# Maxima of a cross-attention's scores in the two row halves of the array, and its weighted sum in one PSUM bank

## The chip, the cores and the metric

One core of one Trainium2 chip. The metric is the device time of one execution in microseconds (us). Three runs of the kernel before took 4037.01, 4039.97 and 4041.73 us; the median is 4039.97.

## The reference

The program is a stack of four layers on `x` (32 batches, 56 tokens, 128 features), each a cross-attention and a feed-forward part; layer 3's cross-attention also has a self-attention ahead of it. All four cross-attentions read the same context `ctx_512` (32 batches, 1500 keys, 64 features), with 16 heads. Cut to what matters, layer 0 is

```
qh = (norm(x) @ Wq) by head;  kh = (ctx @ Wk) by head;  vh = (ctx @ Wv) by head
attn = softmax(qh . kh * scale)          # over 1500 keys
x    = x + (attn . vh) by head @ Wo + bo
x    = x + ffn(norm(x))
```

Layers 1 to 3 differ in head size, biases and in a normalised context (layer 3). The four cross-attentions are called cross 0 to cross 3 here; the kernel's index for them is `ci`.

## The kernel before

**Folding.** `Wk` is folded into `Wq` and `Wv` into `Wo` ahead of each cross-attention, so every head has 64 query features that meet the raw context, and 64 output features. For a batch there are 16 x 56 = 896 rows (head, token), in 7 groups of 128 (`NJ`), and 1500 keys in 12 tiles of 125 (`KT`, `KP`). fp32 values are split into two bf16 halves, high and low.

**Operands of the scores.** The keys of a batch lie in `cs` (128 partitions: 64 high halves above 64 low halves), the high halves once more in `chx` (64 partitions, and a 65th full of ones). The queries lie in `Qh` (high halves, twice, on partitions 0 to 63 and 64 to 127) and `Ql` (64 low halves, and the row's shift, minus its maximum, on the 65th). A score tile, 125 keys by 448 rows, is two matmuls into one bank (L619, L622): `cs` against `Qh` (128 rows), and `chx` against `Ql` (65 rows).

**Maxima.** The softmax's shift needs a rough maximum over the keys for each row. The 1500 keys are taken as three lots of 500, called s, r and the difference d = first lot minus second (`diff`, made by VectorE in `keys`, L777). For each of the 7 groups `product` (L588) makes three 128 x 500 products: d, s and r, 21 in a batch. ScalarE takes relu(d) (`relu`, L687), VectorE adds s to it and takes the maximum in one instruction, which is the larger of the first two lots, and takes the maximum of r by itself (`reduce`, L762). The 7 shifts per row block are turned by TensorE, copied, and sent by DMA to `Ql`'s 65th row.

**Steps.** One stage is a loop over steps `T`, 12 per batch, 384 in all, written out for each engine; every engine takes its work of a step in the order of the code. `turns` (L355) gives the maxima products of a step, for a batch 17 steps ahead, from the table `PLAN` (L359): up to two items, a first and a second. TensorE's order within a step (`pe_cross`, from L602) is: the first product; four score matmuls; the second product; the weighted sum of the tile two steps back; and in some steps a projection of queries (24 matmuls of 56 columns, 32 in cross 2), 7 transposes, or half of the output projection (`slot`, L417). ScalarE: relu of the first item, two exponentials of 125 x 448, relu of the second. VectorE: the first item's maximum, the low halves of the exponentials (L817), the second item's. GpSimd: the rest of these low halves (L539) and the finishing of a batch.

**Banks.** The products take banks 0 and 1 in turn (in a stage's first batch 0 to 3), so that each waits until the last but one has been read (`wait_max_bank`, L401). The scores take banks 2 to 4 in turn. The weighted sum has columns 2620 to 3522, in banks 5 and 6: for each of the 7 groups 129 columns, which are 64 features by the high half, the denominator, and 64 features by the low half. Bank 7 serves the rest.

**Weighted sum** (L628 to L647): for each group one matmul with the high halves of the exponentials as weights and 129 columns of `cnb`, and one with the low halves and 65 columns. The fourth group meets the bank's end at column 3072, so that its 129 columns are cut into 65 and 64: 15 matmuls in all. After the last tile of a batch ScalarE copies the 903 columns to `raw` in two pieces (L724, L725); GpSimd adds the two features' parts, divides, and splits the result into high and low halves (L546 to L564).

**Copies.** SyncE sends a batch's projected queries from `qch` and `qcl` to `Qh` (four DMAs, L389 and L390) and `Ql` (two, L392 and L393); the products wait for the first four, the scores for all six.

Of the kernel before, what the change touches and what calls it, by code (L numbers as in the profile page):

```python
# [22 lines left out]
EPS = 1e-5  # L23
TWICE = 6
E, F = 8, 256
RND = 12582912.0

# [14 lines left out]
def build(nc, a, out):  # L42
    with ExitStack() as ctx:
# [39 lines left out]
        Ql = big[:, 7168:14336].bitcast(BF16).rearrange("p (b n) -> p b n", b=HB)  # L83
        O = big[:, 14336:21504].bitcast(BF16).rearrange("p (b j c) -> p b j c", b=HB, j=NJ)
# [7 lines left out]
        chx = [cx[0:65, 2250 + 750 * i:3000 + 750 * i].bitcast(BF16) for i in range(2)]  # L92
# [5 lines left out]
        raw = [wst[:, 4032 + 903 * i:4935 + 903 * i].rearrange("p (j c) -> p j c", j=NJ) for i in range(2)]  # L98
# [256 lines left out]
        def turns(T):  # L355
            k, n = divmod(T + 17, KT)
            return [(k, PLAN[n])] if 0 <= k < B else []
# [3 lines left out]
        ORDER = tuple(i for two in PLAN for i in two if i)  # L361
        PARTS = {"d": 0, "s": 1, "r": 2}

        def before(item, kinds):
            return sum(i[0] in kinds for i in ORDER[:ORDER.index(item)])

        def halves(kb, item):
            return NJ * kb + before(item, "d")

        def maxima(kb, item):  # L370
            return 2 * NJ * kb + before(item, "sr")

        def products_to(kb, item):
            return len(ORDER) * kb + ORDER.index(item)
# [8 lines left out]
        def sp_spread(y, w, ci, k):  # L383
# [17 lines left out]
        def wait_max_bank(w, kb, k, item):  # L401
            n = ORDER.index(item)
            if k == 0 and n < 4:
                if kb:
                    w.wait_ge(s["red"], maxima(kb, ORDER[0]))
# [1928 lines left out]
```

## Time and profile before

| | |
|---|---|
| time, median of 3 | 4039.97 us |
| profiled execution: span, first to last instruction | 4037.7 us |
| TensorE matmuls, busy | 3793.1 us (94%), 43467 of them |
| TensorE weight loads, busy | 2886.6 us (71%) |
| VectorE, busy | 3135.7 us (78%) |
| ScalarE, busy | 2674.0 us (66%) |
| GpSimd, busy | 2544.9 us (63%) |
| mean granted TensorE clock | 0.954 |

The profiled execution is another one than the three timed; the profile gives its span, and no time of its own beyond that. In the rows below PE is TensorE, PEld its weight loads, DVE VectorE, ACT ScalarE, POOL GpSimd, SPq the DMA queue of SyncE. `ps<-cx,wst` is an instruction that writes `ps` from `cx` and `wst`; `125*128 125x65` is 125 rows by 128 columns of weights, and 65 moving columns on 125 rows; x15 is how many follow one another. A matmul's duration is its latency, not its share of the engine: matmuls overlap, so the distance between two starts is what one takes from TensorE. `[0.20 <-DVE wst L772]` is idle time before the instruction and what ended it. Nearly all matmuls go through the helper at L186, so groups are told apart by their tiles and shapes.

### The profile page before, as it was taken

What the parts mean: (1) busy time and instruction counts of PE and PEld (TensorE: products, weight loads), DVE (VectorE), ACT (ScalarE), POOL (GpSimd) and SP (SyncE); (2) the same over time, 40 slices, a digit from 0 to 9 for tenths busy, and PEclk for the clock granted to TensorE, in tenths of its full rate; (3) what the DMA queues carried; (4) which work ended last, traced back from release to release, by engine and by line L of the source; (5) the groups of instructions that cost most, each with busy time, mean ns of one, the idle gap of its engine ahead of it and who ended that gap; (6) DMA issues with size and microseconds to landing.
All of it is one profiled execution on the core that took longest, in us unless ns stands there. A gap on an engine that the chain in (4) does not pass through costs nothing.

```text
span 4037.7 us, 110587 instructions
## 1 busy us (share of the span) xinstructions
PE 3793.1 (94%) x43467; PEld 2886.6 (71%) x43467; DVE 3135.7 (78%) x6499; ACT 2674.0 (66%) x5365; POOL 2544.9 (63%) x2457
## 2 busy tenths in 40 slices
PE   6999999989969999999799999996997899999987
PEld 4777777766637777777577777775765677777765
DVE  6999999858978888888577888886654788888864
ACT  4888887756637777777467777773442577777752
POOL 4888888759856776767456676675001476676761
PEclk8999999979989999999699999998998899999988
DMA  4333333125432222121112212110000212122100
GB/s 129 104 110 112 110 108 107 41 92 158 143 100 61 57 60 61 54 61 49 28 54 62 59 54 64 57 54 21 3 1 18 64 54 64 57 59 61 55 22 15
DMA packets 157328, 266.80 MB, mean 66 GB/s; under 512 B 26632, under 2 KB 97432, under 8 KB 155432
## 3 DMA queue, kind: packets, MB, share of 16 engines
q1 hardware_dynamic: 156360, 259.67, 22.5%
q8 instruction: 343, 5.62, 0.6%
q14 instruction: 177, 1.45, 0.1%
q10 hardware_dynamic: 448, 0.06, 0.0%
HBM read 165.10 MB, written 50.26 MB: 53 GB/s over the span
## 4 chain that ended last, share of the span: by engine, by line
PE 87%; DVE 6%; POOL 2%; ACT 2%; DMA 1%; issue 1%; SPq 1%; POOLq 0%; DVEq 0%; ACTq 0%
PE ps L186 83%; PE ps L659 1%; DVE xn L166 1%; POOL wst L539 1%; PE ps L242 1%; PE ps L255 1%; PE ps L1638 1%; DVE wst L817 1%; DVE wst L772 0%; PE ps L1160 0%; DVE st L151 0%; DMA big<-big 0%; DVE relu L769 0%; DMA ynN<-cx 0%; ACT wb L324 0%
## 5 line engine op out<-in xcount | busy, mean ns | idle before, releaser
L539 POOL TENSOR_TENSOR wst<-wst 125x384 bf16<-125x384 f32 (+1 forms) x1536 | 1432.0, 932 | 843.4 <-ACT wst L745 783.1
L745 ACT ACTIVATE wst<-ps 125x448 f32<-125x448 f32 x3072 | 1518.5, 553 | 569.3 <-PE ps L186 554.8
L186 PE MATMUL ps<-big,cx 128*125 128x448 bf16 (+1 forms) x6144 | 1428.8, 354 | 0.8 <-DMA big<-topT 0.8
L186 PEld LDWEIGHTS ps<-cx,wst 125*128 125x128 bf16 x23040 | 1113.5, 98 | 307.5 <-POOL wst L539 15.2
L817 DVE TENSOR_TENSOR wst<-wst 125x512 bf16<-125x512 f32 (+1 forms) x1536 | 1269.4, 827 | 56.8 <-ACT wst L745 56.5
L186 PE MATMUL ps<-cx,wst 125*128 125x65 bf16 (+2 forms) x23040 | 1202.4, 204 | 12.1 <-POOL wst L539 11.6
L186 PEld LDWEIGHTS ps<-big,cx 128*125 128x125 bf16 (+1 forms) x6144 | 835.1, 137 | 284.2 <-issue 1.8
L186 PE MATMUL ps<-cx,big 128*128 128x500 bf16 (+1 forms) x2688 | 709.4, 317 | 10.2 <-DVE big L1743 2.6
L772 DVE TENSOR_REDUCE wst<-ps 128x1 f32<-128x500 f32 x896 | 603.9, 674 | 136.6 <-PE ps L186 123.9
L769 DVE CUSTOM_DVE_ANT_0 wst<-ps,wst 128x500 bf16<-128x500 f32 x448 | 302.6, 676 | 207.2 <-PE ps L186 150.8
L769 DVE CUSTOM_DVE_ANT_0 relu<-ps,relu 128x500 bf16<-128x500 f32 x448 | 301.8, 674 | 147.8 <-PE ps L186 84.1
L186 PE MATMUL ps<-diff,big 128*128 128x500 bf16 x896 | 343.5, 383 | 33.7 <-DMA big<-big 20.8
L693 ACT ACTIVATE wst<-ps 128x500 bf16<-128x500 f32 x448 | 270.9, 605 | 67.5 <-PE ps L186 67.5
L693 ACT ACTIVATE relu<-ps 128x500 bf16<-128x500 f32 x448 | 269.2, 601 | 40.5 <-PE ps L186 39.6
L182 POOL TENSOR_TENSOR rs<-ve,mhalf 128x8 f32<-128x8 f32 x26 | 43.1, 1656 | 394.2 <-DVE ve L161 380.3
L186 PEld LDWEIGHTS ps<-cx,big 128*128 128x128 bf16 x2688 | 202.2, 97 | 79.4 <-DVE wst L772 19.4
L564 POOL TENSOR_TENSOR big<-wst,big 128x448 bf16<-128x448 f32 x124 | 173.8, 1402 | 9.7
L186 PE MATMUL ps<-big 128*128 128x448 bf16 (+2 forms) x832 | 162.2, 353 | 4.4 <-POOL big L1055 2.3
L734 ACT ACTIVATE xn<-ps 128x896 bf16<-128x896 bf16 x128 | 122.3, 956 | 49.0 <-PE ps L659 48.4
L546 POOL TENSOR_TENSOR wst<-wst 128x448 f32<-128x448 f32 x124 | 146.0, 1177 | 9.7
L186 PEld LDWEIGHTS ps<-diff,big 128*128 128x128 bf16 x896 | 88.1, 98 | 83.1 <-DMA big<-big 21.4
L552 POOL TENSOR_TENSOR wst<-wst,rden 128x448 f32<-128x448 f32 x124 | 139.9, 1128 | 9.7
(250 smaller groups left out, 4260.2 us busy)
## 6 DMA issues: line engine op xcount, KB each, us to landing
big<-big SPq DMA_DIRECT2D x768, 56.0 KB, 2.7
cx<-ctxT SPq DMA_DIRECT2D x96, 375.0 KB, 3.5
cx<-ctxN SPq DMA_DIRECT2D x64, 377.9 KB
cx<-in_ctxN SPq DMA_DIRECT2D x64, 375.0 KB
cx<-ctxT SPq DMA_DIRECT2D x96, 187.5 KB, 3.8
ctxN<-cx SPq DMA_DIRECT2D x32, 377.9 KB
ynN<-cx SPq DMA_DIRECT2D x32, 377.9 KB
cx<-ynN SPq DMA_DIRECT2D x32, 377.9 KB
```

The costliest lines, as they stand in the source:

```text
L182: g.tensor_tensor(rs[:, cols], ve[:, cols], mhalf[:, cols], ALU.pow).then_inc(s["pw"], 1)
L186: return t.matmul(o, l, r, start=start, stop=stop, skip_group_check=True)
L539: g.tensor_tensor(pl[r][0:KP, at:], pf[r][0:KP, at:], pf[r][0:KP, at:].bitcast(BF16)[:, 1::2], ALU.subtract).then_inc(s["plp"], 1)
L546: g.tensor_tensor(r, r, raw[u][:, :, C + 1:], ALU.add).then_inc(s["fp"], 1)
L552: g.tensor_tensor(r, r, per_row(rden[u][:, :], C), ALU.mult).then_inc(s["fp"], 1)
L564: g.tensor_tensor(O[:, k % HB, :, C:], r, O[:, k % HB, :, 0:C], ALU.subtract).then_inc(s["fp"], 1)
L693: e.activation(relus[n % 2], bank(max_bank(kb, k, item), 500), ACT.Relu).then_inc(s["half"], 1)
L734: e.activation(ob[p % 2][:, :, 64 * r:64 * r + NQ], bank(7).bitcast(BF16)[:, 0:HQ].rearrange("c (h q) -> c h q", h=H), ACT.Copy).then_inc( ...
L745: e.activation(pf[T % 3][0:KP, cols], bank(2 + n2 % 3, 448)[0:KP], ACT.Exp, scale=scale).then_inc(s["ev"], 1)
L769: v.tensor_tensor_reduce(out=half, in0=of, in1=half, scale=1.0, scalar=-3.0e38, op0=ALU.add, op1=ALU.max, accum_out=to[:, j, 0:1]).then_in ...
L772: v.tensor_reduce(to[:, j, 1:2], of, AX.X, ALU.max).then_inc(s["red"], 1)
L817: v.tensor_tensor(pl[r][0:KP, 0:to], pf[r][0:KP, 0:to], pf[r][0:KP, 0:to].bitcast(BF16)[:, 1::2], ALU.subtract).then_inc(s["pl"], 1)
```

## The change

The halves are laid out anew. `cs` holds the high halves of the keys twice, and `chx` zeros with a row of ones on partitions 0 to 63 and the low halves on 64 to 127. `Qh` and `Ql` get the names `Q1` (high above low halves) and `Q2` (shift in partition 0 of a block of zeros, high halves on 64 to 127). The score matmuls become `cs` against `Q1` and `chx` against `Q2`, both with 128 rows. Maxima use only the high halves of the keys: a pair of products runs on 64 rows each, one on partitions 0 to 63 with `Q1`, one on 64 to 127 with `Q2`, into two banks; a product that is alone in its step has 128 rows. `PLAN` has 9 pairs and 3 singles for a batch, all at the start of the step, ahead of the scores; the products take banks 0, 1 and 6 in turn. The weighted sum has 65 columns per group in bank 5 alone, and adds the features' low part onto the same columns by a matmul of its own: 21 matmuls, one copy by ScalarE, no addition by GpSimd. Products wait for all six query copies.

```diff
-        PLAN = (("d0", "s0"), ("r0", "d1"), ("s1", "d2"), ("r1", ""), ("s2", "r2"), ("d3", "s3"),
-                ("r3", "d4"), ("s4", "d5"), ("r4", "s5"), ("r5", "d6"), ("s6", ""), ("r6", ""))
...
+        PLAN = (("d0", "r0"), ("d1", "s0"), ("r1", "r2"), ("d2", "s1"), ("d3", "s2"), ("r3",),
+                ("d4", "s3"), ("d5", "s4"), ("r4", "r5"), ("d6", "s5"), ("s6",), ("r6",))
...
+        TILES = (slice(0, 64), slice(64, 128))
...
-        def max_bank(kb, k, item):
-            n = products_to(kb, item)
-            return n % 2 if k else ORDER.index(item) % 4
...
+        def max_bank(k, n, u):
+            return (0, 1, 6)[(through(n - 1, "dsr") + u) % 3] if k else 2 * (n % 2) + u
...
-            for r in (0, 64):
-                y.dma_start(Qh[r:r + 64, o, 0:HQ // 2], qch[u][0:64]).then_inc(s[f"qd_{u}"], 16)
-                y.dma_start(Qh[r:r + 64, o, HQ // 2:], qch[u][64:128]).then_inc(s[f"qd_{u}"], 16)
+            for of, rows in ((Q1, TILES[0]), (Q2, TILES[1])):
+                y.dma_start(of[rows, o, 0:HQ // 2], qch[u][0:64]).then_inc(s[f"qd_{u}"], 16)
+                y.dma_start(of[rows, o, HQ // 2:], qch[u][64:128]).then_inc(s[f"qd_{u}"], 16)
...
-            y.dma_start(Ql[0:64, o, 0:HQ // 2], qcl[u][0:64]).then_inc(s[f"ql_{u}"], 16)
-            y.dma_start(Ql[0:64, o, HQ // 2:], qcl[u][64:128]).then_inc(s[f"ql_{u}"], 16)
+            y.dma_start(Q1[64:128, o, 0:HQ // 2], qcl[u][0:64]).then_inc(s[f"ql_{u}"], 16)
+            y.dma_start(Q1[64:128, o, HQ // 2:], qcl[u][64:128]).then_inc(s[f"ql_{u}"], 16)
...
                 if k < B:
-                    y.dma_start(cs[i], srcT[k]).then_inc(s[f"lT_{i}"], 16)
+                    for rows in TILES:
+                        y.dma_start(cs[i][rows, :], srcT[k][0:64]).then_inc(s[f"lT_{i}"], 16)
...
-            for k in range(2):
-                g.memset(chx[k][64:65, :], 1.0).then_inc(s["zo"], 1)
-                w.wait_ge(s["zo"], zeroed(ci - 1) + k + 1)
+            if ci in (0, 3):
+                g.memset(cx[0:64, 2250:3750], 0.0).then_inc(s["zo"], 1)
+                w.wait_ge(s["zo"], zeroed(ci - 1) + 1)
+                g.memset(cx[0:1, 2250:3750], ONES).then_inc(s["zo"], 1)
+                w.wait_ge(s["zo"], zeroed(ci - 1) + 2)
...
+            g.memset(big[0:64, 7168:7168 + QB * HQ // 2], 0.0).then_inc(s["zo"], 1)
...
-                if 0 <= (k := due(T, KT + 4)) < B - 1:
-                    u, kb = k % 2, B * ci + k
-                    r = raw[u][:, :, 0:C]
-                    w.wait_ge(s["fc"], 2 * (kb + 1))
-                    g.tensor_tensor(r, r, raw[u][:, :, C + 1:], ALU.add).then_inc(s["fp"], 1)
-                    w.wait_ge(s["fp"], 4 * kb + 1)
...
-            def product(k, item):
-                kind, j = item[0], int(item[1])
+            def products_of(k, n):
+                items = PLAN[n]
                 wait_spread_high(w, ci, k)
+                wait_spread_low(w, ci, k)
                 wait_keys(w, ci, k)
                 w.wait_ge(s["dif"], b0 + k + 1)
-                wait_max_bank(w, b0 + k, k, item)
-                c = PARTS[kind]
-                mm(t, bank(max_bank(b0 + k, k, item), 500), Qh[:, k % QB, 128 * j:128 * j + 128],
-                   diff[:, :] if kind == "d" else cs[k % 3][:, 500 * c:500 * c + 500], True, True).then_inc(s["mxm"], 1)
+                wait_max_banks(w, b0 + k, k, n)
+                for u, item in enumerate(items):
+                    c, j = PARTS[item[0]], int(item[1])
+                    rows = TILES[u] if len(items) == 2 else slice(0, 128)
+                    r = mm(t, bank(max_bank(k, n, u), 500), (Q1, Q2)[u][rows, k % QB, 128 * j:128 * j + 128],
+                           diff[rows, :] if c == 0 else cs[k % 3][rows, 500 * c:500 * c + 500], True, True)
+                r.then_inc(s["mxm"], len(items))
 
...
                     n2 += 1
-                for k, items in turns(T):
-                    if items[0]:
-                        product(k, items[0])
+                for k, n in turns(T):
+                    products_of(k, n)
...
                         w.wait_ge(s["ev"], evac + n2 - 2)
-                        mm(t, o, cs[k % 3][:, keys], Qh[:, k % QB, cols], True, False)
+                        mm(t, o, cs[k % 3][:, keys], Q1[:, k % QB, cols], True, False)
                         wait_shift(w, ci, k)
-                        wait_spread_low(w, ci, k)
-                        mm(t, o, chx[k % 2][:, keys], Ql[0:65, k % QB, cols], False, True).then_inc(s["sc"], 1)
+                        mm(t, o, chx[k % 2][:, keys], Q2[:, k % QB, cols], False, True).then_inc(s["sc"], 1)
                         n2 += 1
-                for k, items in turns(T):
-                    if items[1]:
-                        product(k, items[1])
                 if 0 <= T - 2 < NT:
                     k, i = divmod(T - 2, KT)
                     r = (T - 2) % 3
                     ph = pf[r][0:KP, :].bitcast(BF16)[:, 1::2]
                     w.wait_ge(s["pl"], t0 + T - 1)
                     wait_values(w, ci, k)
-                    if k:
-                        w.wait_ge(s["fc"], 2 * (b0 + k) - 1)
+                    w.wait_ge(s["fc"], b0 + k)
                     for j in range(NJ):
-                        if k and j == 3:
-                            w.wait_ge(s["fc"], 2 * (b0 + k))
                         if j == JP[ci]:
                             w.wait_ge(s["plp"], NT * ci + T - 1)
                         cols = slice(128 * j, 128 * j + 128)
-                        at = 2620 + 129 * j
-                        n = min(129, 3072 - at) if at < 3072 else 129
-                        mm(t, ps[:, at:at + n], ph[:, cols], cnb[k % 3][:, i, 0:n], i == 0 and j == 0, False)
-                        if n < 129:
-                            mm(t, ps[:, at + n:at + 129], ph[:, cols], cnb[k % 3][:, i, n:129], i == 0, False)
+                        at = ACC + 65 * j
+                        mm(t, ps[:, at:at + 65], ph[:, cols], cnb[k % 3][:, i, 0:C + 1], i == 0 and j == 0, False)
+                        mm(t, ps[:, at:at + C], ph[:, cols], cnb[k % 3][:, i, C + 1:], False, False)
                         r_ = mm(t, ps[:, at:at + 65], pl[r][0:KP, cols], cnb[k % 3][:, i, 0:65], False, i == KT - 1)
                     r_.then_inc(s["pv"], 1)
                 what, p, k = slot(T)
...
-                    e.activation(whole[:, 0:452], ps[:, 2620:3072], ACT.Copy).then_inc(s["fc"], 1)
-                    e.activation(whole[:, 452:], ps[:, 3072:2620 + 129 * NJ], ACT.Copy).then_inc(s["fc"], 1)
+                    e.activation(whole, ps[:, ACC:ACC + 65 * NJ], ACT.Copy).then_inc(s["fc"], 1)
```

## Rows read from the trace of the kernel before

**Rows 1.** part 4 of the page: the chain of work that ended last, by line
```profile
PE ps L186 83%; PE ps L659 1%; DVE xn L166 1%; POOL wst L539 1%; PE ps L242 1%; PE ps L255 1%; PE ps L1638 1%; DVE wst L817 1%; DVE wst L772 0%; PE ps L1160 0%; DVE st L151 0%; DMA big<-big 0%; DVE relu L769 0%; DMA ynN<-cx 0%; ACT wb L324 0%
```
**Rows 2.** what TensorE waited for in the whole span: us, times, longest
```profile
PE ps L186 <- DMA big<-big: 20.8, 4, 15.9
```
**Rows 3.** busy time by stretch, cross 0 and cross 1, both in mid-stage
```profile
110.00:740.00 630.00, 628.93 (x8095) 488.00 (x8096) 578.65 (x1048) 507.08 (x1038) 523.14 (x546) 1.00 0.39 108
1300.00:1800.00 500.00, 500.00 (x6464) 390.44 (x6463) 406.20 (x836) 376.73 (x783) 349.68 (x348) 1.00 0.21 60
```
**Rows 4.** longest pieces of the chain in cross 1: start us, us, what
```profile
1425.00 39.84 PE ps L186 x517
1471.05 39.84 PE ps L186 x517
```
**Rows 5.** groups by form: busy us, mean ns of one, idle before
```profile
L186 PE MATMUL ps<-cx,wst 125*128 125x129 bf16 x9216 | 1153.0, 221 | 12.1 <-POOL wst L539 11.6
L186 PE MATMUL ps<-cx,wst 125*128 125x65 bf16 x12288 | 1110.1, 193 | 0.0
```
**Rows 6.** TensorE in order of time, two steps of cross 1: start us, us
```profile
1499.84 0.92 PE L186 MATMUL ps<-big,cx 128*125 128x448 bf16 x4
1500.61 0.78 PE L186 MATMUL ps<-cx,wst 125*128 125x129 bf16 x15
1501.22 0.78 PE L186 MATMUL ps<-xT,wa 128*128 128x56 bf16 x24
1501.85 0.37 PE L186 MATMUL ps<-diff,big 128*128 128x500 bf16 x1
1502.06 0.73 PE L186 MATMUL ps<-big,cx 128*125 128x448 bf16 x3
```
**Rows 7.** the same within the weighted sum, from its seventh and its tenth matmul
```profile
1500.87 0.40 PE L186 MATMUL ps<-cx,wst 125*128 125x65 bf16 x6
1500.96 0.39 PE L186 MATMUL ps<-cx,wst 125*128 125x129 bf16 x5
```
**Rows 8.** TensorE where 128-row matmuls give way to 8-row ones, full clock
```profile
866.67 1.68 PE L186 MATMUL ps<-big 128*128 128x448 bf16 x8
868.28 0.48 PE L186 MATMUL ps<-wst,big 8*128 8x128 f32 x2
868.49 1.05 PE L186 MATMUL ps<-wst,big 8*128 8x128 f32 x8
```
**Rows 9.** TensorE where 8-row matmuls give way to 128-row ones, half clock
```profile
828.71 1.27 PE L255 MATMUL ps<-big 8*64 8x128 f32 x5
829.91 0.69 PE L193 MATMUL ps<-idf,xn 128*128 128x128 f32 x2
```
**Rows 10.** TensorE, bf16 gives way to fp32 with all 128 rows kept
```profile
2894.43 0.65 PE L186 MATMUL ps<-cx,big 128*128 128x56 bf16 x19
2894.92 0.39 PE L1638 MATMUL ps<-idf,big 128*68 128x128 f32 x2
```
**Rows 11.** TensorE, a 500-column matmul after a wait, and the next
```profile
48.97 0.39 PE L186 MATMUL ps<-diff,big 128*128 128x500 bf16 x1 [0.20 <-DVE wst L772]
49.19 0.37 PE L186 MATMUL ps<-cx,big 128*128 128x500 bf16 x1
```
**Rows 12.** last query copy of a batch, mid-stage; then the start of cross 2
```profile
1497.79 0.60 SPq L393 DMA_DIRECT2D big<-big  x1
big<-big SPq DMA_DIRECT2D x156, 56.0 KB, 2.7
2011.31 0.60 SPq L393 DMA_DIRECT2D big<-big  x1
2012.09 0.60 PE L186 MATMUL ps<-diff,big 128*128 128x500 bf16 x1 [1.32 <-DMA big<-big]
```
**Rows 13.** GpSimd at the start of cross 0
```profile
21.55 2.74 POOL L513 MEMSET cx<- 1x1500 bf16 x2 [2.78 <-PE ps L193]
24.98 1.80 POOL L518 MEMSET xn<- 128x2048 f32 x1
```

More of the change, by code:

```diff
@@ L356, in turns, with first, through, group_of @@
             k, n = divmod(T + 17, KT)
-            return [(k, PLAN[n])] if 0 <= k < B else []
-        PLAN = (("d0", "s0"), ("r0", "d1"), ("s1", "d2"), ("r1", ""), ("s2", "r2"), ("d3", "s3"),
-                ("r3", "d4"), ("s4", "d5"), ("r4", "s5"), ("r5", "d6"), ("s6", ""), ("r6", ""))
-        ORDER = tuple(i for two in PLAN for i in two if i)
+            return [(k, n)] if 0 <= k < B else []
+        PLAN = (("d0", "r0"), ("d1", "s0"), ("r1", "r2"), ("d2", "s1"), ("d3", "s2"), ("r3",),
+                ("d4", "s3"), ("d5", "s4"), ("r4", "r5"), ("d6", "s5"), ("s6",), ("r6",))
+        ORDER = tuple(i for group in PLAN for i in group)
         PARTS = {"d": 0, "s": 1, "r": 2}
-        def before(item, kinds):
-            return sum(i[0] in kinds for i in ORDER[:ORDER.index(item)])
-        def halves(kb, item):
[L368 to L374, printed above, removed]
-        def max_bank(kb, k, item):
-            n = products_to(kb, item)
-            return n % 2 if k else ORDER.index(item) % 4
+        TILES = (slice(0, 64), slice(64, 128))
+        def first(count, kinds):
+            return sum(i[0] in kinds for i in ORDER[:count])
+        def through(n, kinds):
+            return sum(i[0] in kinds for group in PLAN[:n + 1] for i in group)
+        def group_of(item):
+            return next(n for n in range(KT) if item in PLAN[n])
+        def halves(kb, item):
+            return NJ * kb + int(item[1])
+        def maxima(kb, n):
+            return 2 * NJ * kb + through(n, "sr")
+        def products(kb, n):
+            return len(ORDER) * kb + through(n, "dsr")
+        def max_bank(k, n, u):
+            return (0, 1, 6)[(through(n - 1, "dsr") + u) % 3] if k else 2 * (n % 2) + u
         def place(h):
@@ L399, in wait_spread_low, with wait_max_banks @@
             w.wait_ge(s[f"ql_{k % 2}"], 32 * (B // 2 * ci + k // 2 + 1))
[L401 to L405, printed above, removed]
-                return
-            b4, of = (kb, ORDER[n - (2 if k else 4)]) if n >= 2 else (kb - 1, ORDER[n - 2])
-            if k == 1 and n < 2:
-                w.wait_ge(s["red"], maxima(kb, ORDER[0]))
-            elif of[0] == "d":
-                w.wait_ge(s["half"], halves(b4, of) + 1)
-            else:
-                w.wait_ge(s["red"], maxima(b4, of) + 1)
+        def wait_max_banks(w, kb, k, n):
+            done = through(n, "dsr") - 3 if k else through(n - 2, "dsr") if n >= 2 else 0
+            if k == 1 or done >= 0:
+                w.wait_ge(s["half"], NJ * kb + first(max(done, 0), "d"))
+                w.wait_ge(s["red"], 2 * NJ * kb + first(max(done, 0), "sr"))
+            else:
+                w.wait_ge(s["half"], NJ * (kb - 1) + first(len(ORDER) + done, "d"))
+                w.wait_ge(s["red"], 2 * NJ * (kb - 1) + first(len(ORDER) + done, "sr"))
         QSLOT = {1: ("project", 2), 2: ("high", 2), 3: ("low", 2), 6: ("project", 3), 7: ("high", 3), 8: ("low", 3)}
@@ L685, in high, with relu @@
                 e.activation(qch[k % 2], bank(7, 448), ACT.Copy).then_inc(s["pa"], 1)
[L687 to L693 removed]
+            def relu(k, n):
+                kb, item = b0 + k, PLAN[n][0]
+                w.wait_ge(s["mxm"], products(kb, n))
+                h, j = halves(kb, item), int(item[1])
+                if h >= 2:
+                    w.wait_ge(s["red"], maxima(kb, group_of(f"s{j - 2}")) if j >= 2 else maxima(kb - 1, group_of(f"s{j + NJ - 2}")))
+                e.activation(relus[h % 2], bank(max_bank(k, n, 0), 500), ACT.Relu).then_inc(s["half"], 1)
             high(0)
@@ L735, in act_cross @@
                                  ACT.Copy).then_inc(s["oc"], 1)
[L736 to L738 removed]
+                for k, n in turns(T):
+                    if PLAN[n][0][0] == "d":
+                        relu(k, n)
                 if 0 <= T < NT:
```

101 lines of the change are left out of this document (47 added, 54 removed).

## The prediction

> **What bounds the kernel now.** I read the chain of waits first. TensorE's line for all ordinary matmuls holds 83% of the span [rows 1], and in cross 1 it runs through TensorE in pieces of 39.84 us that start 46.05 us apart, two batches [rows 4], so a batch takes 23.0 us and a step 1.92. Then the busy times by stretch: in mid-stage TensorE is busy 500.00 of 500 us in cross 1 and 628.93 of 630 in cross 0; VectorE, next, has 406 of 500 (81%) in cross 1 and 579 of 630 (92%) in cross 0, ScalarE 377 of 500 [rows 3]. The list of waits says the same: of the idle time before maxima products that is put down to the query copies, 20.8 us in all, there are four cases, the stage starts, the longest 15.9 [rows 2]. So in the four cross stages (128 batches of 12 steps, 1536 steps) only what changes the distance between two matmul starts moves the time. Busy time does not show that: a 65-column matmul counts 193 ns and a 129-column one 221 [rows 5], yet 15 of them start within 0.61 us. I therefore work with starts.
>
> **Prices now, as distances between starts** [rows 6]. A 500-column product: 2.06 - 1.85 = 0.21 us. Four score matmuls of 448 columns: 0.77, so 0.19 each. The weighted sum: 1.22 - 0.61 = 0.61 for 15 matmuls with 7 x 129 + 7 x 65 = 1358 columns. Projection: 24 matmuls of 56 columns in 0.63, so 0.026 each. At 2.4 GHz (the granted clock is 1.00 there [rows 3]) 56 columns are 0.023; about 3 ns come on top of each matmul. That fits the weighted sum: 566 ns of columns + 15 x 3 = 611.
>
> **Part A, products in pairs.** 21 products a batch become 9 pairs and 3 singles. If the halves of a pair run side by side, one slot of 0.21 goes per pair, 9 x 128 = 1152 times: -242 us. What comes in is that the array is used as two 64-row halves for the pair and as one of 128 rows for what stands on either side of it. The trace has no pair, but it has changes of the row count. Eight 448-column matmuls end, by their modelled ends, at 866.67 + 1.68 = 868.35, and the first 8-row one begins at 868.28, 0.07 before [rows 8]; in the other direction, at half clock, the end is 829.98 and the next begins at 829.91, again 0.07 before [rows 9]. Without such a change a matmul begins long before the end of the last: the 65-column ones end at 1501.39 and the projection begins at 1501.22, 0.17 before; a product ends at 1502.22 and the next begins at 1502.06, 0.16 before [rows 6]. It isn't the data type: from bf16 to fp32 with all 128 rows the run ends at 2895.08 and the next begins at 2894.92, 0.16 before [rows 10]. So a change costs 0.10 after a weighted sum and 0.09 after a product, and each pair has two, going in and coming out.
> The weights that come first after the change aren't loaded ahead. A product that starts after a wait shows this price in bf16: 0.39 instead of 0.37, and 0.22 to the next instead of 0.21 [rows 11], so 0.01. Coming out, the first weights are the 125-column ones of the scores; I take 0.02, with 0.01 [rows 11] and 0.10 as bounds (the fp32 load after the change: 0.21 to the next start instead of 0.11 [rows 8]).
> How far the second half starts behind the first no row shows: 0 at best, 0.21 at worst (one after the other). I take 0.026, the shortest distance at which TensorE starts matmuls with their own weights [rows 6], since the other half of the array is free.
> Sum per pair: -0.21 + 0.10 + 0.01 + 0.026 + 0.09 + 0.02 = +0.036 us; x 1152 = **+41 us**. The gain is eaten by the two changes.
> On the change of mode the Trainium skill (TensorEngine Tiling (Array Packing), Key Properties) says that changing the tiling mode drains TensorE; the 0.07 above agrees, and without that drain the sum would be rival 1. For the second half the skill (TensorE: Matmul & The Clock Gate, Measured speedup vs the span model) gives about 4 ns per tile, which no row here shows; the pair would then cost +0.014 and part A +16 us, an estimate from that page.
>
> **Part B, weighted sum in one bank.** Per step 15 matmuls become 21 of 65, 64 and 65 columns, the columns stay 1358. Six more at 3 ns: +18 ns, x 1536 = **+28 us**. Bounds: one of the seven column groups is already cut like that (it meets the bank's end), and its three start within 1500.96 - 1500.87 = 0.09 [rows 7]; 7 x 0.09 = 0.63 against 0.61, which is the value taken. Read with the 0.005 of rounding at each end, 0.085 to 0.095 gives -15 to +55 ns a step, -23 to +84 us. Such short matmuls are not limited by their issue: 24 of them at 0.026 follow directly on the 15 [rows 6].
>
> **Part C, waits and starts.** Maxima products now wait for the copies of the low query half too. In mid-stage the last of these is issued at 1497.79 and takes 2.7 us, to 1500.5 [rows 12]; the batch's first product is at 1501.85 [rows 6]: covered by 1.3 us, paid only if copies get that much slower. At a stage start it isn't covered: in cross 2 the first product begins at 2012.09, on the landing of the high copies, while the last low one was issued at 2011.31 [rows 12], and with 2.7 us to landing it comes 1.9 later: 4 x 1.9 = +8 us, at most. GpSimd's memsets at the start of cross 0 lose two one-row fills (2.74) and gain some 3000 to 5700 columns at 1.80 / 2048 = 0.9 ns [rows 13]: 1500 + 1500 + 2688 columns = 5.0, so +2.3 us, since its next work follows at once. In the other stages GpSimd is done before TensorE needs it, by my reading. **+10 us** together, 0 to 10.
> At nothing: the removed addition on GpSimd and the one ScalarE copy instead of two, as both engines have slack [rows 3]; the larger score contraction (65 rows become 128), since a slot goes by columns: the 128-row and the 65-row score matmuls together take 4 x 0.19 [rows 6]; two key loads instead of one, same bytes. The weighted sum of the next batch waits for one copy of 0.58 us instead of the first of two, and is about 1 us behind the step's start in TensorE's order, behind the scores. Banks: a pair needs what its last but one predecessor's bank held, which an engine took up one step (1.92 us) earlier, with 0.67 of work; queued behind a pair that waits are the scores, exponentials and everything else, so this is where a new stall would come from.
>
> **Sum.** 41 + 28 + 10 = +79 us. The profiled execution has a span of 4037.7; the median is 4039.97, 2.3 above it, and I add to the median: **4119 us**, 2.0% slower.
>
> **Rivals.**
> 1. The change of row halves costs little in bf16 (all rows for it involve fp32). Then a pair gives 0.21 - 0.026 = 0.184 back: -212 us, with B and C +38: 3866. VectorE would allow it: it is busy 92% of cross 0 [rows 3], 21.2 us of a batch of 23.0, and TensorE would need 23.0 - 1.7 + 0.3 = 21.6. For it: both row counts are loaded by the same kind of instruction. Against it: the same 0.07 in both directions and at both clocks [rows 8, 9]. It decides from 0.09 per change (-0.21 + 0.026 + 2 x 0.09 = 0): below 0.075 per change the gain exceeds B and C, and the kernel is faster. Half of the price, 0.05 each without load cost, gives 1152 x -0.084 = -97 + 38: 3981. Chance of this side 0.19.
> 2. The halves don't run side by side. Then the second costs 0.21 instead of 0.026: +212 us on the forecast, 4331. For it: no row shows two matmuls at once. Against it: they share neither rows nor a bank. 0.10.
> 3. Bank and release stalls: a product is released only with its pair, 0.1 to 0.2 later, and VectorE in cross 0 has only 8% of slack [rows 3]. 0.2 us in each of cross 0's 384 steps is +77: 4196. 0.08.
> 4. All unknowns at their cheap ends (second half at 0, loads at 0.01, B and C at 0): -0.21 + 0.10 + 0.01 + 0 + 0.09 + 0.01 = 0, so 4040: no change. 0.08.
> The forecast has 0.55, with 4050 to 4190 as its own range.
>
> **How the numbers follow.** A difference under 0.2% (8 us) can't be told from none here. Faster takes rival 1 and nothing else, 0.19; the same takes rival 4, 0.08; the rest is slower, 0.73. The range reaches down to 4000, into rival 1's weak form, and up to 4230, over rival 3 and the dear ends of B; it leaves out rival 2 and most of rival 1, and of the rest little.
>
> **What would show it.** In the changed profile: the two 500-column matmuls of a pair some 0.03 us apart (0.21 says rival 2); the next score matmul starting 0.07 before the pair's end, 0.3 after its start (0.21 says rival 1), and the pair starting 0.07 before the end of the weighted sum; 21 weighted-sum matmuls in about 0.63; TensorE busy less than 100% or unchanged, with no wait on VectorE or ScalarE above a few us (else rival 3); the first product of a stage a little over 1 us later behind the query copies. The forecast is wrong if TensorE's batch in mid-stage gets shorter than the 23.0 us it has now.

## The result and the profile after

The changed kernel takes **4091.17 us** (median of 4 runs, 4089.79 to 4093.36) beside 4040.72 for the kernel before (4 runs, 4037.01 to 4041.73): **1.0128 of it, 95% interval 1.0114 to 1.0143**, some 50 us slower. The profiled execution has a span of 4089.3 us against 4037.7.

No new kind of wait has come in. The page's chain (share of the span by line) has the line of the ordinary matmuls, now L189, at 85% where [rows 1] had 83%. The list of waits puts one stage start down to the landing of query copies where [rows 2] had four; the other three now stand under "issue", a wait that the profile puts down to nothing (they end at 43.49, 2037.65 and 3194.66 us, each at the first product of a stage):

```profile
PE ps L189 85%; PE ps L657 1%; POOL wst L549 1%; DVE xn L169 1%; PE ps L245 1%; PE ps L1633 1%; PE ps L1155 0%; PE ps L258 0%; DVE st L154 0%; DMA big<-big 0%; DVE wst L771 0%; DMA ynN<-cx 0%; PE ps L196 0%; ACT wb L327 0%; POOL big L568 0%
...
PE ps L189 <- DMA big<-big: 17.5, 1, 17.5
PE ps L189 <- issue: 7.5, 3, 2.6
...
PE ps L189 <- POOL wst L549: 4.5, 10, 0.5
```

The same two stretches as in [rows 3] show TensorE without a gap. VectorE and ScalarE have 2 to 3% less to do in 500 us than before, because the batches have become 2.4% longer (ScalarE also has one copy less); GpSimd falls from 350 to 285, because its addition is gone (columns: PE, PEld, DVE, ACT, POOL busy, clock, DMA share, GB/s):

```profile
110.00:740.00 630.00, 630.00 (x9883) 476.84 (x9881) 575.64 (x1027) 494.02 (x990) 459.60 (x509) 1.00 0.40 107
1300.00:1800.00 500.00, 500.00 (x7829) 378.67 (x7828) 397.78 (x817) 366.58 (x742) 285.07 (x318) 1.00 0.22 58
```

So the loss is in distances between starts. Here is one step with a pair, from TensorE's timeline, matmuls and weight loads (start us, us); it answers to [rows 6]:

```profile
1500.73 0.57 PEld L189 LDWEIGHTS ps<-big,cx 128*125 128x125 bf16 x4 [0.22 <-ACT wst L742]
1500.73 0.97 PE L189 MATMUL ps<-big,cx 128*125 128x448 bf16 x4
1501.54 0.81 PE L189 MATMUL ps<-cx,wst 125*128 125x65 bf16 x21
1502.28 0.38 PE L189 MATMUL ps<-diff,big 64*128 64x500 bf16 x1
1502.29 0.38 PE L189 MATMUL ps<-cx,big 64*128 64x500 bf16 x1
1502.60 0.97 PE L189 MATMUL ps<-big,cx 128*125 128x448 bf16 x4
```

Read it from below. The halves of the pair start 0.01 apart: they do run side by side. The next score matmul starts 0.31 after the pair, not 0.21. Its weights are loaded only then; the first line shows this for the pair before, where the load engine had been idle for 0.22 when the load began at 1500.73, together with the score matmul. The four scores take 1501.54 - 1500.73 = 0.81 instead of 0.77. The weighted sum takes 1502.28 - 1501.54 = 0.74 instead of 0.61, and the change into the pair is in it. Both changes keep the 0.07 of [rows 8, 9]: the weighted sum ends at 1501.54 + 0.81 = 1502.35 and the pair starts at 1502.28, the pair ends at 1502.67 and the score matmul starts at 1502.60.

The timeline rounds to 10 ns, so I summed the record's start-to-start distances in nanoseconds. Such a distance, from a matmul's start to the next one's, is called its slot here. Each slot is booked on the matmul that begins it; the change into a pair is therefore booked on what stands ahead of the pair. Mean of 22 batches of cross 1 (the 7th to the 28th), ns in a batch, for this kernel and for the experiments below:

```
                  scores  products  weighted  projec-  transposes,   batch
                                    sum       tion     output
before              9169     4482      7400      624      1348       23023
after               9531     3468      8380      716      1485       23580
e9  128-row scores  9058     4459      7420      624      1348       22909
e10 one bank        9186     4470      7754      623      1344       23377
e1  full rows       9066     4440      7764      623      1344       23238
e7  wide keys       9218     3486      8380      716      1484       23285
e8  fours           9849     2851      8193      669      1494       23056
e12 relu later      9550     2851      8269      669      1494       22834
```

After less before is +557 ns in a batch, x 128 = +71 us, against +51.6 of span. Of the 20 that are missing, 4 are stalls of cross 0 that are gone (its batch was 23152 ns, not 23023), 4 lie outside the four stages (a stage is counted from its first to its last score matmul), and about 12 in the first and last batches of the stages: from its first to its last score matmul the last one takes 18.5 us instead of 19.95 (19.2 in cross 0).

### The profile page after: what moved, and what is told of

Same layout as the page of the kernel before. It is cut to its first block, busy times and chain, and to the rows that moved or that the text cites. A ratio compares the mean times of both kernels' runs of the same rounds, so it can differ in the third digit from the quotient of the medians.

```text
span 4089.3 us, 129408 instructions
## 1 busy us (share of the span) xinstructions
PE 3842.1 (94%) x52683; PEld 2867.7 (70%) x52683; DVE 3151.5 (77%) x6495; ACT 2666.9 (65%) x5237; POOL 2254.6 (55%) x2333
## 4 chain that ended last, share of the span: by engine, by line
PE 88%; DVE 4%; POOL 2%; ACT 2%; DMA 2%; issue 1%; SPq 1%; POOLq 0%; DVEq 0%; ACTq 0%
PE ps L189 85%; PE ps L657 1%; POOL wst L549 1%; DVE xn L169 1%; PE ps L245 1%; PE ps L1633 1%; PE ps L1155 0%; PE ps L258 0%; DVE st L154 0%; DMA big<-big 0%; DVE wst L771 0%; DMA ynN<-cx 0%; PE ps L196 0%; ACT wb L327 0%; POOL big L568 0%
## 5 line engine op out<-in xcount | busy, mean ns | idle before, releaser
L549 POOL TENSOR_TENSOR wst<-wst 125x384 bf16<-125x384 f32 (+1 forms) x1536 | 1292.5, 841 | 1202.5 <-ACT wst L742 1167.0
L189 PE MATMUL ps<-big,cx 128*125 128x448 bf16 x6144 | 1475.8, 363 | 0.9 <-DMA big<-topT 0.9
L189 PEld LDWEIGHTS ps<-cx,wst 125*128 125x128 bf16 x32256 | 1198.9, 98 | 228.3 <-POOL wst L549 6.3
L189 PE MATMUL ps<-cx,wst 125*128 125x65 bf16 (+1 forms) x32256 | 1244.8, 193 | 5.1 <-POOL wst L549 4.5
L189 PEld LDWEIGHTS ps<-big,cx 128*125 128x125 bf16 x6144 | 743.9, 136 | 437.4 <-ACT wst L742 189.9
L189 PE MATMUL ps<-cx,big 64*128 64x500 bf16 (+2 forms) x2688 | 627.5, 323 | 12.7 <-DVE wst L771 4.3
L189 PE MATMUL ps<-diff,big 64*128 64x500 bf16 x896 | 351.1, 393 | 44.8 <-DMA big<-big 17.5
L189 PEld LDWEIGHTS ps<-cx,big 64*128 64x128 bf16 (+1 forms) x2688 | 172.3, 94 | 51.4 <-ACT wst L691 13.1
L189 PE MATMUL ps<-big 128*128 128x448 bf16 (+2 forms) x832 | 163.1, 355 | 4.0 <-POOL big L1050 1.8
L189 PEld LDWEIGHTS ps<-diff,big 64*128 64x128 bf16 x896 | 83.0, 93 | 110.8 <-issue 18.5
L189 PE MATMUL ps<-wb,xn 128*128 128x128 bf16 x2048 | 140.2, 224 | 4.0 <-ACT xn L731 4.0
```

Source lines behind the costliest of these rows:

```text
L189: return t.matmul(o, l, r, start=start, stop=stop, skip_group_check=True)
L549: g.tensor_tensor(pl[r][0:KP, at:], pf[r][0:KP, at:], pf[r][0:KP, at:].bitcast(BF16)[:, 1::2], ALU.subtract).then_inc(s["plp"], 1)
```

## Experiments

Ratios are against the kernel before on the same chip. Its median is 4040.4 to 4041.8 us on each of the chips used, so medians from different chips are set side by side below.

**e1: no halves.** All else of the changed kernel is kept.

```
-                    rows = TILES[u] if len(items) == 2 else slice(0, 128)
-                    r = mm(t, bank(...), (Q1, Q2)[u][rows, k % QB, ...],
+                    rows = slice(0, 128)
+                    r = mm(t, bank(...), Q1[rows, k % QB, ...],
```


> The changed kernel with both products of a pair on all 128 rows (so one after the other), all else kept. Theory: in mid-stage a pair in halves costs 33 ns more than two slots of 213 (95 going in, 3 between the halves, 311 to the next start, 51 on the first score matmul behind it, against 426). Then 1152 x -33 ns = -38 us: 4053, and the first score matmul after a product takes 0.19 again. Rival: the pairs are even and the rise comes from the weighted sum and the new order of the step; then 4091, unchanged. Rival 1 of the prediction (the halves save time): above 4091.

Measured: 4062.29 us, ratio 1.0052 (1.0035 to 1.0069), 29 us less than the changed kernel. In mid-stage 342 ns of a batch go, 38 per pair, x 1152 = 44 us. But the way from a stage's first product to its first score matmul, run at half clock in part and waiting for banks, takes 19.4 us instead of 17.3 (in cross 0 21.0 instead of 18.7), 9 us in all: there the halves pay. The spans differ by 28.9: 42 less in the stages, 9 more on these ways, and 4 more in the rest, where the edit changes nothing.

```profile
1500.83 0.81 PE L189 MATMUL ps<-cx,wst 125*128 125x65 bf16 x21
1501.48 0.38 PE L189 MATMUL ps<-diff,big 128*128 128x500 bf16 x1
1501.69 0.37 PE L189 MATMUL ps<-cx,big 128*128 128x500 bf16 x1
1501.90 0.92 PE L189 MATMUL ps<-big,cx 128*125 128x448 bf16 x4
1502.66 0.53 PE L189 MATMUL ps<-cx,wst 125*128 125x65 bf16 x12
```

Two products cost 0.42, the scores 0.76, and the weighted sum ahead (1500.83 to 1501.48) 0.65: all three prices of the pair are gone, and so is its gain.

**e10: the weighted sum in one bank alone**, put into the kernel before.

```
-                        mm(t, ps[:, at:at + n], ph[:, cols], cnb[...][:, i, 0:n], ...)
-                        ...
+                        mm(t, ps[:, at:at + 65], ph[:, cols], cnb[...][:, i, 0:C + 1], ...)
+                        mm(t, ps[:, at:at + C], ph[:, cols], cnb[...][:, i, C + 1:], False, False)
```


> The kernel before with the weighted sum of the changed kernel and nothing else of it: one PSUM bank, 21 matmuls of 65, 64 and 65 columns in a step instead of 15 of 129, 129 and 65, no addition on GpSimd. Theory (29 ns more in a step, and 1.5 us less in the last batch of each of four stages): 1536 x 0.029 = +45, -6, so 4080 us. Rival P (the 3 ns per added matmul that the prediction took, 18 ns in a step): +28 - 6, so 4063 us. Rival Q (the slots of the weighted sum grow only beside the pairs or the 128-row scores): 4035 to 4045 us.

Measured: 4068.83 us, 1.0067 (1.0053 to 1.0081), +27 us with 21 to 33 around it. The total is near rival P's, but by another sum. Mid-stage the weighted sum does cost 354 ns more in a batch, 29.5 in a step, +45 us. In the profile 12 come back within the stages: 4 as stalls of cross 0 (its batch grows by 215 ns only), 8 in the first and last batches (the last 18.61 us instead of 19.95). There TensorE does wait for GpSimd, which no longer makes the addition: all the 11.6 us of [rows 5] lie in the last two batches of a stage, and here it is 3.6. Outside the stages 9.5 come back, of which the runs explain 3.7: the very last batch is finished by VectorE, with one operation less, and TensorE waits less for it, 9.7 as in the changed kernel (us, times, longest; before, then the changed kernel):

```profile
PE ps L659 <- DVE big L809: 13.4, 4, 3.4
PE ps L657 <- DVE big L806: 9.7, 4, 2.4
```

The rest is the profiled execution's own: it took 4063.37 us, the other three 4068.72 to 4071.03, and 7.5 of the 9.5 lie between cross 0 and cross 1, where a DMA landed earlier too.

**e9: 128-row scores alone**, in the kernel before.

```
-                        mm(t, o, chx[k % 2][:, keys], Ql[0:65, k % QB, cols], False, True)
+                        mm(t, o, chx[k % 2][:, keys], Ql[:, k % QB, cols], False, True)
```


> The kernel before with one edit: the second matmul of the scores contracts 128 rows instead of 65 (63 rows of zeros in keys and queries). Theory (in the score matmuls, slots of 192 to 194 ns go to 189 where a 65-row matmul no longer stands between 128-row ones): 8 ns less in a step, x1536 = -12 us, plus some 2 us of GpSimd zeroing at stage starts: 4030 us, the score matmuls of a batch at about 9070 ns instead of 9169. Rival (the short slots of the changed kernel came from its order of work, not from the rows): 4041 to 4043 us.

Measured: **4027.00 us, 0.9965 (0.9953 to 0.9978)**: faster than both kernels. The batch is 114 ns shorter, 111 of them in the scores. In the kernel before, the slot of a 128-row score matmul is 188.4 ns behind a 128-row product and 191.6 behind a 65-row matmul, and a product's is 213.3 behind a 65-row matmul, 210.8 in e9: the slot behind another row count is the longer one. The timeline of e9 (start us, us) has the four in 0.76:

```profile
1500.70 0.92 PE L186 MATMUL ps<-big,cx 128*125 128x448 bf16 x4
1501.46 0.37 PE L186 MATMUL ps<-diff,big 128*128 128x500 bf16 x1
```

**e5: the reverse**, the second score matmul of the changed kernel back on 65 rows.

```
-                        mm(t, o, chx[k % 2][:, keys], Q2[:, k % QB, cols], False, True)
+                        mm(t, o, chx[k % 2][0:65, keys], Q2[0:65, k % QB, cols], False, True)
```


> The changed kernel whose second score matmul contracts 65 rows instead of 128 (63 of the 64 low halves of the keys' part are left out). Theory: the 448-column slots fell from 191 to 189 ns since both score matmuls have the same row count; then the old 191 comes back, 8 ns x 1536 = +12 us: 4103. Rival: the row count has no part in it: 4091. If a change between 65 and 128 rows cost as much as one between 64 and 128, it would be over +300 us, which the kernel before already speaks against.

Measured: 4111.19 us, 1.0173 (1.0157 to 1.0188). The scores of a batch go from 9531 to 9642 ns, slots from 189 to between 192 and 193. The weighted sum gives 18 ns back, so the batch is 95 ns longer, the 12 us of the theory. The spans differ by 21; of the other 9 us 4 lie in the first and last batches and 5 outside the stages, where the edit changes nothing. Their cause stays open.

**e6: products behind the scores**, so that the way out of a pair leads into 128-column weights.

```
-                for k, n in turns(T):
-                    products_of(k, n)
                 if 0 <= T < NT:
                     ... scores ...
+                for k, n in turns(T):
+                    products_of(k, n)
```


> The changed kernel with the products behind the scores and ahead of the weighted sum (relu behind the exponentials, maxima behind the low halves). Same work, but the first weights after a pair are 128 columns wide instead of 125. Theory: the 51 ns that the first score matmul loses after a pair are its slow 125-column weight load that isn't hidden; behind a pair the weighted sum's load costs about 5. So -46 ns x 1152 = -53 us: 4038, and the slot after the pair stays 311. Rival a: the 51 belong to the change of rows itself and move along: 4091. Rival b: relu and maxima come 0.8 us later in the step and TensorE waits for banks: above 4091, with waits of TensorE on VectorE or ScalarE in the list.

Measured: 4079.11 us, 1.0095 (1.008 to 1.011), a gain of 12 where 53 were expected. The 46 ns per pair were saved, and then paid again in part: the first score matmul now stands right behind the short ones of the weighted sum or a projection, and holds 216 to 219 ns instead of 189, nine times a batch. The other three times it stands behind 128-column matmuls (transposes or the output projection, slots of 56 ns), and holds 190.5. That the load of the 125-column weights costs the 27 ns fits, as it takes 136 ns and one of 128 columns 97; but e6 was not run with 128 columns. In the timeline of this kernel (start us, us) the scores that follow a weighted sum directly and precede a pair take 0.88, 0.03 at their beginning and 0.09 for the change at their end:

```profile
1500.90 0.95 PE L189 MATMUL ps<-big,cx 128*125 128x448 bf16 x4
1501.78 0.38 PE L189 MATMUL ps<-diff,big 64*128 64x500 bf16 x1
```

**e7: 128 key columns as weights** instead of 125 for eleven of a batch's twelve tiles; the three results more aren't used.

```
+                    wide = 128 if i < KT - 1 else KP
-                    keys = slice(KP * i, KP * i + KP)
+                    keys = slice(KP * i, KP * i + wide)
```


> The changed kernel whose score matmuls load 128 columns of keys instead of 125 (three more rows of the bank are written and not read), but for a batch's last tile. Theory: the 51 ns on the first score matmul after a pair are the slow load of 125 columns; 128 columns load four times as wide and cost about 5 ns there. 8 of a batch's 9 pairs stand before such a tile: 1024 x -46 ns = -47 us: 4044. Rival: the 51 ns belong to the change of row halves, whatever is loaded: 4091.

Measured: 4063.91 us, 1.0056 (1.0041 to 1.0071), 27 us less than the changed kernel. The batch is 294 ns shorter, which would be 38 us; in the spans 33 of them show in the stages, and outside the stages 4 are added, where the edit changes nothing. The first score slot after a pair is 201 ns instead of 240, with the same 448 moving columns: of the 51 ns that this load cost, 39 hung on the three missing weight columns.

```profile
1501.45 0.38 PE L189 MATMUL ps<-cx,big 64*128 64x500 bf16 x1
1501.76 0.93 PE L189 MATMUL ps<-big,cx 128*128 128x448 bf16 x4
1502.53 0.66 PE L189 MATMUL ps<-cx,wst 125*128 125x65 bf16 x16
```

**e8: e7 with two pairs in a row**, so that two changes serve four products; this takes four banks for products and leaves two for scores.

```
+        PLAN = (("d0", "r0"), ("d1", "r1"), ("s0", "r2"), ("d2", "s1"), ("d3", "s2"), ("d4", "r3"),
+                ("s3", "r4"), ("d5", "s4"), ("d6", "s5"), ("r5", "s6"), ("r6",))
+        STEPS = ((0, 1), (), (2, 3), (), (4, 5), (), (6, 7), (), (), (8, 9), (10,), ())
-                        o = bank(2 + n2 % 3, 448)[0:wide]
+                        o = bank(2 + n2 % 2, 448)[0:wide]
```


> The same, and the pairs joined to fours: 20 of a batch's 21 products in 5 steps of two pairs each, the last alone, in banks 0, 1, 6 and 4, with the scores in two banks (2 and 3) instead of three. Theory (what costs is going into the halves and out, not the halves): a four costs 95 + 3 + 210 + 3 + 311 + 5 = 0.63 us against four slots of 213 = 0.85. Per batch 9 x 0.415 + 3 x 0.212 = 4.37 becomes 5 x 0.63 + 0.21 = 3.36, -1.01 us x 128 = -130 us under e7_wide_keys: about 3914, 3% under the kernel before. VectorE is then busy some 96% in cross 0. Rival: a four needs four banks read and the scores have two, so TensorE waits for VectorE or ScalarE, 0.1 to 0.2 us in each of 640 steps with a four or more: 3980 to 4050.

Measured: 4043.91 us (10 runs), 1.0011 (1.0001 to 1.002), 20 us less than e7. Products, weighted sum and projection together give 870 ns in a batch, as fewer changes for the same products should; but the scores lose 631, and in three places. In every second batch's third step TensorE waits 466 ns for ScalarE's copy of the one accumulator bank; in every second batch's seventh step it waits 360 ns in cross 1 and 1.31 us in cross 0 for VectorE's low halves; in each ninth step 214 ns for one of the two score banks. The first and the third of these in the timeline (start us, us, engine):

```profile
1479.00 0.59 ACT L695 ACTIVATE relu<-ps 128x500 bf16<-128x500 f32 x1
1479.47 0.57 ACT L726 ACTIVATE wst<-ps 128x455 f32<-128x455 f32 x1
1480.18 0.80 PE L189 MATMUL ps<-cx,wst 125*128 125x65 bf16 x21 [0.30 <-ACT wst L726]
...
1491.54 0.59 ACT L695 ACTIVATE wst<-ps 128x500 bf16<-128x500 f32 x1
1492.01 0.25 ACT L718 ACTIVATE topT<-ps 7x128 bf16<-7x128 f32 x1
1492.30 1.15 ACT L745 ACTIVATE wst<-ps 125x448 f32<-125x448 f32 x2
1492.31 0.11 PEld L189 LDWEIGHTS ps<-big,cx 128*128 128x128 bf16 x2 [0.49 <-ACT topT L718]
```

Both begin with a relu (L695) that ScalarE does first, and behind it the small copy for which TensorE, in the end, waits.

**e11: e8 with ScalarE's other copies behind the exponentials.**

```
-                what, p, k = slot(T)
-                ... high(k), turned copy ...
                 ... exponentials ...
+                what, p, k = slot(T)
+                ... high(k), turned copy ...
```


> The kernel with products in fours with one edit: ScalarE's copies of the projected queries and of the turned output stand behind the step's two exponentials instead of ahead of them. In the kernel with fours the score matmuls wait for a bank where a relu and one of these copies stand ahead of the exponentials: 421 instead of 189 ns in step 2 of a batch, 370 in step 6 and 215 more in that step's weighted sum, 400 in step 8 (which has another copy and stays). Theory (order on ScalarE causes the stalls): 300 to 600 ns less in a batch of some 23050, x128 = -38 to -77 us, so about 3985 us, with 3965 to 4006 around it. Rival (VectorE, busy 84% of the stretch, is the limit whose waiting only shows there): the waits move to other steps and the time stays within 10 us of 4044.

Measured: 4067.15 us, 1.0068 (1.0053 to 1.0084), 23 slower than e8. The theory falls: the slots of the third and the seventh step stay at 422 and 369 ns, and the ninth's wait grows from 214 to 635 ns in every second batch, because a query copy that is put off now stands ahead of the next step's relu and of the small copy of the maxima (L718), for which that step waits. The waits of TensorE's weight loads for this copy, from 1300 to 1800 us (us, times, longest), in e8 and then in e11:

```profile
PEld ps L189 <- ACT topT L718: 10.8, 22, 0.5
PEld ps L189 <- ACT topT L718: 14.5, 21, 0.9
```

Reading the lines of e8 once more showed what does stand ahead there, in the third step and in the ninth: the relu.

**e12: e8 with the second pair's relu one step later**, behind those copies.

```
+                for k, n in turns(T - 1)[1:]:
+                    relu(k, n)
                 ... query and output copies, first pair's relu, exponentials ...
-                for k, n in turns(T)[1:]:
-                    relu(k, n)
```


> The kernel with products in fours (4044 us) with one edit: the relu of a step's second pair is issued by ScalarE one step later, behind that step's copy of the accumulator bank and of the maxima, ahead of its exponentials. In the trace of the kernel with fours, TensorE's weighted sum in every second batch's third step waits 466 ns for the accumulator copy, which began at 1479.47, right behind a relu that began at 1479.00; and the third score matmul of each ninth step waits 214 ns for exponentials behind a copy of the maxima at 1492.01 that stands behind such a relu (1491.54). Theory (these relus in front of ScalarE's urgent copies cause two of the three stalls, 233 + 211 ns in the mean batch): x128 = -57 us, so 3987 us, with 3975 to 4010 around it; the third stall (VectorE's low halves, seventh step) stays. Rival (ScalarE only passes the wait on, so the exponentials come later by the relu and the scores or the weighted sum wait for them instead): 4034 to 4054 us.

Measured: **4014.32 us, 0.9927 (0.9913 to 0.994)**, 30 less than e8 and **faster than both kernels**. The fourth score slot of the third step goes from 422 to 257 ns in the mean batch and the ninth step's wait is gone; but half of the 444 ns expected isn't gained: 68 stay in that slot, 66 come back in the third step's weighted sum and some 90 in the eleventh step. 222 ns in a batch are left. The wait for VectorE's low halves stays as it was (all waits of TensorE for it, us, times, longest; 27.7 and 63 in e8):

```profile
PE ps L189 <- DVE wst L815: 28.3, 65, 1.2
```

**e3 and e4: why three short matmuls cost 92.5 ns.** The slots in a group of three are 30.0, 32.8 and 29.7 ns, 4.5 above three equal ones of 29.3, which is what most 65-column slots take. e3 takes contiguous weights for the high half, e4 begins the second matmul at an even column.

```
-                    ph = pf[r][0:KP, :].bitcast(BF16)[:, 1::2]            (e3)
+                    ph = pl[r][0:KP, :]
-                        mm(t, ps[:, at:at + C], ph[:, cols], cnb[...][:, i, C + 1:], False, False)   (e4)
+                        mm(t, ps[:, at:at + C], ph[:, cols], cnb[...][:, i, C:2 * C], False, False)
```


> The changed kernel whose weighted sum uses the contiguous low halves of the exponentials as weights in all 21 matmuls, in place of the high halves read at a step of 4 bytes (the high part of the sum is left out). A weighted sum takes 0.647 us in the changed kernel, 92.5 ns for 65, 64 and 65 columns, while matmuls behind low-half weights take 29. Theory S (the strided weights make the slots long): 21 x 29.2 = 613, -34 ns x 1536 = -52 us: 4039. Rival M (the odd start of the moving columns, or the plain number of matmuls): no change, 4091.

> The changed kernel whose second matmul of each group in the weighted sum streams columns 64 to 127 of the values' block instead of 65 to 128 (the low part of the last feature is replaced; sum shifted by one column). In the changed kernel the tiles differ: in even tiles the 64-column slot is 33 to 34 ns and the other two 29, in odd tiles about 31, 32 and 29; a tile's block begins at 129 x i columns of 2 bytes, so which start is a multiple of 4 bytes goes by tile. Theory O (a moving operand that doesn't start on 4 bytes costs some 4 ns): even tiles then have no such start, 7 x 4.5 = 32 ns less in half of the steps, so -25 us: 4066, if odd tiles keep theirs. Rival (the matmuls' number or their adding onto the same columns): 4091, unchanged.

Measured: 4092.64 us (1.0128) and 4094.20 us (1.0132), the changed kernel's time; the slots of e3 are 30.0, 32.7 and 29.7. The stride of the weights isn't the cause. The start column only moves the split: in odd tiles the three go from 30.1, 31.9 and 30.1 to 29.9, 34.1 and 29.2, and the sum doesn't fall. What makes one slot of three 32 to 34 ns stays open. The three add onto overlapping columns of the bank, but in the kernel before the cut group's 64 columns lie in another bank than the 65 ahead of them, and that slot is 33.0 too.

## Why the prediction was right, and where its terms were not

Predicted +79 us (4119), measured +50; slower, inside the range and inside the forecast's own 4050 to 4190.

- **Pairs, predicted +41.** The mechanism is shown: the pair runs side by side and both changes are paid. From the record, per pair: 112 ns less on the products' own slots; +95 for the change in (124 ns instead of 29 after a 65-column matmul), where 0.10 and 0.01 stood; the slot out 311 ns instead of 213, so +98 where 0.09 stood; the second half 3 ns behind the first, where 26 was taken; and the first scores' load +51, where 20 was taken. -213 + 3 + 98 + 95 + 51 = +34, x 1152 = +39 us. That 39 meets 41 is luck: the second half was 23 ns too dear and the load 31 too cheap, the change in 15 too dear and the one out 8 too cheap. 0.026 was a distance between matmuls on the same rows, which says nothing of another half of the array, and [rows 11], from which the load's lower bound came, has 128 columns of weights. For the second half the Trainium skill (TensorE: Matmul & The Clock Gate, Measured speedup vs the span model) had the size right, about 4 ns per tile; here it is 3.3. For the rest my reading of 0.07 before the end in [rows 8, 9] was enough, though those changes involved fp32.
- **Rivals 1 and 2** fall by the same lines: 0.31 out of the pair, 0.01 between its halves. **Rival 3** falls with TensorE's full stretches. It came true in e8, with two score banks. **Rival 4** had the second half right but needed the cheap load, and the weighted sum at nothing.
- **Weighted sum, predicted +28.** Alone it measures +27, with 21 to 33, and that too is luck: the term was mis-sized and so was an item put at nothing. It is 29.5 ns in a step and not 18 (+45 us). The size was lost in the rounding of [rows 6, 7]: the group read as 0.09 takes 93.6 ns in the record and 92.5 in the changed kernel, so seven take 0.65 and not 0.63. Against it stand some 16 us that come back within the stages and at their ends. "Both engines have slack" was read from mid-stage, and the removed addition pays where a stage ends: of the 11.6 us of [rows 5] behind GpSimd 4.5 are left.
- **Larger score contraction, put at nothing: -14 us** (e9, with 9 to 19). I reasoned by columns and read 4 x 0.19 from [rows 6], where 2 to 3 ns of a slot can't be seen. 65-row matmuls between 128-row ones are a change of row count as well, at 3 ns and not at 95.
- **Waits and starts, predicted +10: about -4.** Outside the stages each stretch is 0.3 to 1.8 us shorter. The wait for the low copies is there all the same, as foretold: in cross 2 the first product starts 2.87 us after the last projection matmul, not 1.55, and 2.1 after the last low copy is issued (start us, us):

```profile
2035.54 0.60 SPq L402 DMA_DIRECT2D big<-big  x1
2037.65 0.57 PE L189 MATMUL ps<-diff,big 64*128 64x500 bf16 x1 [2.64 <-issue]
```

In cross 3 it is 2.74 instead of 1.46 and in cross 1 17.74 instead of 16.10, but there kernels without this wait scatter too (e9 has 2.65 in cross 3, e10 13.8 in cross 1); in cross 0 nothing changes. So some 1 to 4 us were paid. The shorter stage ends, which the prediction had at nothing, hide them.

Put together from the runs: +27 (e10) - 14 (e9) = 4054; e1, which has both and the new order, is at 4062; the remaining 8 are about its stage starts, which take 1.0 us longer than before in cross 0 and 2.1 to 2.2 in the others; and the halves add 29 (e1 to the changed kernel). 4062 + 29 = 4091.

What pays at once is the by-product, e9 (0.9965). In mid-stage the halves pay nothing in pairs. The kernel gets faster than before (0.9927) once two pairs share a change, the weights behind the change have 128 columns, and ScalarE's order follows the new places of the waits; e8, without the last of these, was no faster than before. What the halves alone give in e12 isn't shown, as that kernel wasn't run with its products on all rows, and e9, with no halves at all, is within 13 us of it.

## What to carry to other kernels

Work in halves of the array that stands between work on all rows pays for two changes of rows, and one pair of 500-column matmuls does not earn them: 213 ns gained, 193 for the changes and up to 51 for weights that could not be loaded ahead. Put several pairs behind one change, and then follow the banks this takes to the engine that frees them. Where TensorE is full, compare distances between starts by kind of neighbour, to the nanosecond, since a display in steps of 10 ns hid 12 ns a step here, 18 us; and read an engine's slack at the end of a stage too, not only in its middle.

## What was not expected of the hardware

- Score matmuls of 448 columns start 189 ns apart when all use 128 rows and some 191 to 193 when 65-row ones alternate with them (e9, e5).
- A score matmul with weights of 125 columns holds 27 ns more behind matmuls of 56 or 65 columns (e6) and 51 more behind a pair; with 128 weight columns the latter is 12 (e7). Behind 128-column matmuls it is 1.5 (e6), and behind a 500-column product on all rows nothing: e9 has 125 columns and 189 ns.
- The change of halves costs 93 to 96 ns into a pair, whether a 65-column, a 56-column, a 128-column or a 448-column matmul stands ahead, and 98 out of it, at full clock and in bf16.
